# Edge attention on one Trainium2 core: one operand of VectorE in PSUM, edge loads spread over other rounds, and one multiplication of the counting loop given to GpSimd

## What is computed

```python
h = jnp.einsum('ni,hio->hno', x, W)                      # 4 heads of 64
e = attn_src[:, src_idx] + attn_dst[:, dst_idx]
e = jnp.where(e >= 0, e, NEG_SLOPE * e) * edge_weight[None, :]
e_exp = jnp.exp(e - jnp.max(e))
denom = jax.ops.segment_sum(e_exp.T, dst_idx, num_segments=num_nodes).T
alpha = e_exp / (denom[:, dst_idx] + 1e-10)
msg = h[:, src_idx] * alpha[..., None]
out = jax.vmap(lambda m: jax.ops.segment_sum(m, dst_idx, num_segments=num_nodes))(msg)
x = x + out                                              # summed by destination, added to x
```

## Time and profile before

| what | value |
|---|---|
| time, median of 3 runs | 5204.59 us (5191.33 to 5204.67) |
| the profiled execution's own time | 5195.46 us |
| its span, first to last instruction | 5193.8 us |
| TensorE busy | 4168.2 us (80%) |
| VectorE busy | 2408.1 us (46%) |
| GpSimd busy | 862.5 us (17%) |
| mean granted TensorE clock | 0.883 |

### The profile page before, as it was taken

The page is one execution under the profiler, slowest core; times in us unless marked ns, Lnnn a source line. Parts: engine busy times, 40 slices in busy tenths (PEclk is TensorE's granted clock), DMA queues, the critical chain, the costliest instruction groups (busy, mean ns, idle before and its releaser), DMA issues. The chain is left out here.

```text
span 5193.8 us, 79246 instructions
## 1 busy us (share of the span) xinstructions
PE 4168.2 (80%) x22693; PEld 3605.1 (69%) x22694; DVE 2408.1 (46%) x4239; ACT 1855.3 (36%) x3178; POOL 862.5 (17%) x796
## 2 busy tenths in 40 slices
PE   2588877955749976967997998997499969899675
PEld 2476767954638843866886886886499858788554
DVE  5355558965340032126995995897411140110424
ACT  2333323642410032424664664665143310110322
POOL 2577770002600010210000000000122200000101
PEclk8688888986969988988998998998599979999788
DMA  3344432542343211321221221221312144133000
GB/s 102 84 114 116 121 90 98 214 172 64 107 140 148 86 33 38 125 72 41 57 54 33 58 57 32 54 56 24 91 60 80 51 132 159 75 150 148 13 18 27
DMA packets 459231, 440.36 MB, mean 85 GB/s; under 512 B 347128, under 2 KB 411341, under 8 KB 446050
## 3 DMA queue, kind: packets, MB, share of 16 engines
q1 hardware_dynamic: 423868, 341.36, 21.6%
q0 software_dynamic: 35232, 97.61, 6.5%
HBM read 342.44 MB, written 96.42 MB: 84 GB/s over the span
## 5 line engine op out<-in xcount | busy, mean ns | idle before, releaser
L2575 PE MATMUL p_acc<-p_H,p_eT 125*125 125x256 f32 x3750 | 823.6, 379 | 0.0
L2575 PEld LDWEIGHTS p_acc<-p_H,p_eT 125*125 125x125 f32 x3750 | 696.2, 187 | 105.0
L1120 POOL DMA_INDIRECT p_message<-edge_table,p_index x425 | 495.1, 1165 | 170.5 <-issue 119.5
L1371 PE MATMUL p_acc<-p_message,p_spread 125*125 125x260 f32 x1666 | 427.9, 424 | 33.9 <-issue 29.1
L2059 DVE BATCH_NORM_STATS2 features_stats<-F x60 | 29.2, 487 | 868.0 <-ACT F L2050 867.3
L1371 PEld LDWEIGHTS p_acc<-p_message,p_spread 125*125 125x125 f32 x1666 | 349.9, 212 | 104.1 <-issue 36.2
L1830 ACT ACTIVATE p_hid<-p_up,p_b1s 128x125 f32<-128x125 f32 x764 | 272.2, 365 | 398.4 <-PE p_up L1806 355.0
L1806 PEld LDWEIGHTS p_up<-p_xT,p_w1s 128*128 128x128 f32 x3056 | 377.6, 199 | 50.1 <-issue 33.8
L1806 PE MATMUL p_up<-p_xT,p_w1s 128*128 128x125 f32 x3056 | 385.0, 284 | 32.0 <-issue 14.0
L1814 PE MATMUL p_down<-p_w2s,p_hid 128*125 128x256 f32 x1528 | 361.3, 386 | 11.7 <-ACT p_hid L1830 10.5
L526 PE MATMUL p_turned<-identity,p_slot 125*128 125x125 f32 x400 | 89.1, 376 | 303.3 <-DVE p_slot L494 299.7
(11 more groups left out here) (492 smaller groups left out, 6794.8 us busy)
## 6 DMA issues: line engine op xcount, KB each, us to landing
sums_first<-edge_sums SPq DMA_DIRECT2D x39, 1562.5 KB
p_count<-edge_counts SPq DMA_DIRECT2D x375, 152.6 KB
p_second<-edge_sums SPq DMA_DIRECT2D x36, 1562.5 KB, 8.0
edge_sums<-p_sums SPq DMA_DIRECT2D x25, 1562.5 KB
edge_counts<-p_total SPq DMA_DIRECT2D x25, 683.6 KB
p_w1s<-in_L_ffn_W SPq DMA_DIRECT2D x16, 1024.0 KB
p_got<-made SPq DMA_DIRECT2D x25, 560.0 KB
p_dst_all<-dst_row SPq DMA_DIRECT2D x25, 531.2 KB
```

Source lines behind the costliest of these rows:

```text
L1120: pool.indirect_dma_start(message[:, m, k, :], None, table, bass.IndirectOffsetOnAxis(ap=index[:, m, k:k + 1], axis=0)).then_inc(landed[m] ...
L1371: last = pe.matmul(at, spread[:, k], message[0:P, m, k], start=(k == 0), stop=(k == R_CH - 1))
L2575: last = pe.matmul(acc[:, s, 0:C], eT[:, r % 4, a % 4], H[:, a, 0:C], start=(a == 0), stop=(a == T - 1))
```

## The change

The change has these parts. (a) In `attend_edges` VectorE reads one operand of L1255 and L1283 from PSUM: the destinations are copied there once (`dst_of`), and ScalarE writes the exponentials a second time, to `raise_of`. (b) SP issues the block loads of a round three rounds later, behind that round's `dst_all`; there are 660 instead of 630. (c) `begin_rest`, `pick_rest`, the first six steps and the last six of `block_keys` stand behind rounds 18, 19, 21 and 22. (d) The two closing instructions over 125 x 6400 are gone; in the counting loop VectorE does the same for one tile of 256 features behind every fifth batch, through `attended`. (e) In the counting loop `heavy` is computed by GpSimd, and `low` is 125 wide instead of 128. (f) The last loop loads and stores 5 columns for each of 25 slices of `old_sums` instead of whole rows.

```diff
-LOADED = 21
-HELD = LOADS * LOADED
+SETS = 3
+HELD = LOADS * ((CH // (CH // T)) - SETS)
...
+def block_lows(dve, then, own):
+
+
+    then(dve.tensor_copy(own.spare, own.edges[:, 0:BLOCKS, 1]))
     then(dve.tensor_scalar(own.base, own.spare, 4195.0, None, ALU.mult))
     then(dve.tensor_copy(own.spare_i, own.base))
     then(dve.tensor_scalar(own.spare_i, own.spare_i, 19, None, ALU.arith_shift_right))
     then(dve.tensor_copy(own.base, own.spare_i))
     then(dve.scalar_tensor_tensor(out=own.low, in0=own.base, scalar=-float(P), in1=own.spare, op0=ALU.mult, op1=ALU.add))
-    then(dve.tensor_copy(own.spare, dst))
+
+
+def block_keys(dve, then, own, based):
+
+
+    then(dve.tensor_copy(own.spare, own.edges[:, 0:BLOCKS, 0]))
...
-        low = ph.sb("low", [EB, SLOTS, KB, ROWS])
+        low = ph.sb("low", [EB, SLOTS, KB, P])
...
+        old_sums = ph.sb("old_sums", [P, T, BLK])
...
-        old_sums = sums[0:P, 1]
...
-            eng.tensor_tensor(heavy[:, at], low[:, at], own.edges[:, bass.ds(n * KB, KB), 2:3].bitcast(F32).to_broadcast([EB, KB, ROWS]),
+            eng.tensor_tensor(heavy[:, at, :, 0:P], low[:, at], own.edges[:, bass.ds(n * KB, KB), 2:3].bitcast(F32).to_broadcast([EB, KB, P]),
                               ALU.mult).then_inc(heavy_ready, 1)
+
+        @block.gpsimd
+        def _(pool):
+            over_batches(pool, lambda n, k, i: weighs(pool, n, k))
 
 
         @block.vector
         def _(dve):
             dve.sem_inc(batch_summed, SLOTS)
+            dve.memset(heavy[:].rearrange("p s b l -> p (s b) l")[:, :, P:ROWS], 0.0).then_inc(cleared, 1)
             dve.sem_inc(counts_kept, TURNS)
             dve.sem_inc(batch_kept, TURNS)
 
...
-                dve.tensor_tensor(low[:, at], lanes(ROWS), each(own.low, n, ROWS), ALU.is_equal).then_inc(low_ready, 1)
+                dve.tensor_tensor(low[:, at], lanes(P), each(own.low, n, P), ALU.is_equal).then_inc(low_ready, 1)
                 dve.tensor_tensor(cell[:, at], lanes(P), each(own.key, n, P), ALU.is_equal).then_inc(cell_ready, 1)
-                weighs(dve, n, k)
-
-            over_batches(dve, one)
...
+
+            def one_and_tile(n, k, i):
+                one(n, k, i)
+                if k % IN_GROUP == IN_GROUP - 1:
+                    t = i * (PER // IN_GROUP) + k // IN_GROUP
+                    o = attended[0][:, tile(t), 0:C].rearrange("p a (h o) -> p (a h) o", h=HEADS)
+                    dve.tensor_tensor(o, o, attended[1][:, tile(t), :].rearrange("p a h -> p (a h)").unsqueeze(2).to_broadcast([P, HEADS, HO]), ALU.mult).then_inc(shared, 1)
+                    dve.wait_ge(shared, t + 1)
+                    x = X[:, tile(t), :].rearrange("p a c -> p (a c)")
+                    dve.tensor_tensor(x, x, attended[0][:, tile(t), 0:C].rearrange("p a c -> p (a c)"), ALU.add)
+
+            over_batches(dve, one_and_tile)
...
+                then(dve.tensor_tensor(old_sums[:], old_sums[:],
                                        acc[0:P, 0, 1, 0, 0:P].rearrange("p (d h) -> p h d", h=T), ALU.add))
...
+                old = weights.rearrange("r (h d) -> r h d", h=T)[bass.ds(group * ROWS, P), :, bass.ds(place * BLK, BLK)]
+                sp.dma_start(old_sums[:], old).then_inc(old_loaded, 16)
...
+                sp.dma_start(old, old_sums[:]).then_inc(rest_stored, 16)
...
-        total = ph.sb("total", [P, T, W])
-        den = ph.sb("den", [P, T, HEADS])
+        total, den = attended
...
+        dst_of = ph.psum("dst_of", [P, 512])
+        raise_of = ph.psum("raise_of", [P, 512])
...
-            with eng.Fori(0, ROUNDS // SETS - 1) as i:
+        def over_pipeline(eng, one, single=1):
+            with eng.Fori(0, ROUNDS // SETS - single) as i:
...
-            for r in range((ROUNDS // SETS - 1) * SETS, ROUNDS):
+            for r in range((ROUNDS // SETS - single) * SETS, ROUNDS):
...
             sp.wait_ge(loops_made, 4)
-            for r in range(SETS):
-                blocks_of(r)
-            with sp.Fori(1, LOADED // SETS) as i:
+            with sp.Fori(1, ROUNDS // SETS) as i:
                 for m in range(SETS):
                     one(i * SETS + m, i, m)
-                    blocks_of(i * SETS + m)
-            for r in range(LOADED, ROUNDS):
+                    blocks_of((i - 1) * SETS + m)
+            for r in range(ROUNDS // SETS * SETS, ROUNDS):
                 one(r, r // SETS, r % SETS)
+                blocks_of(r - SETS)
...
-                act.activation(message[0:P, m, :, C:W], logit[:], ACT.Exp, bias=minus[:, m:m + 1]).then_inc(raised, 1)
+                act.activation(message[0:P, m, :, C:W], logit[:], ACT.Exp, bias=minus[:, m:m + 1])
+                act.activation(raise_of[:, 0:R_CH * HEADS], logit[:].rearrange("p k h -> p (k h)"), ACT.Exp, bias=minus[:, m:m + 1]).then_inc(raised, 1)
...
+            dve.tensor_copy(dst_of[:, 0:CH + PAD], g.dstf[:]).then_inc(dst_kept, 1)
+            dve.wait_ge(dst_kept, 1)
...
                     dve.tensor_tensor(spread[:, lo:lo + n], g.iota[:, nodes(t)].unsqueeze(1).to_broadcast([P, n, P]),
-                                      g.dstf[:, bass.ds(r * R_CH + lo, n)].unsqueeze(2).to_broadcast([P, n, P]),
+                                      dst_of[:, bass.ds(r * R_CH + lo, n)].unsqueeze(2).to_broadcast([P, n, P]),
                                       ALU.is_equal).then_inc(spread_ready, 1)
...
                     o = rows_of[:, :, 0:C].rearrange("p k (h o) -> p k h o", h=HEADS)
-                    dve.tensor_tensor(o, o, rows_of[:, :, C:W].unsqueeze(3).to_broadcast([P, n, HEADS, HO]), ALU.mult).then_inc(scaled, 1)
+                    dve.tensor_tensor(o, o, raise_of[:, lo * HEADS:(lo + n) * HEADS].rearrange("p (k h) -> p k h", h=HEADS).unsqueeze(3).to_broadcast([P, n, HEADS, HO]), ALU.mult).then_inc(scaled, 1)
...
+            rest_then = Steps(dve, rest_setup)
...
                 one(r, i, m, coming)
-                then = Steps(dve, rest_setup, 0 if coming == 2 else 16)
+                if coming == 6:
+                    begin_rest(dve, rest_then, g, own_blocks.low[0:1], own_blocks.spare_i[0:1], own_blocks.spare[0:1, 0:1])
+                if coming == 5:
+                    pick_rest(dve, rest_then, g, own_blocks.low[0:1])
+                if coming == 3 and isinstance(r, int):
+                    dve.wait_ge(own_edges_loaded, 16 * HELD)
+                    block_lows(dve, rest_then, own_blocks)
                 if coming == 2:
-                    over = own_blocks.low[0:1]
-                    begin_rest(dve, then, g, over, own_blocks.spare_i[0:1], own_blocks.spare[0:1, 0:1])
-                    pick_rest(dve, then, g, over)
-                if coming == 1:
-                    dve.wait_ge(own_edges_loaded, 16 * HELD)
-                    block_keys(dve, then, own_blocks, based)
-
-            over_pipeline(dve, one_and_blocks)
+                    block_keys(dve, rest_then, own_blocks, based)
+
+            over_pipeline(dve, one_and_blocks, single=2)
...
-            o = total[:, :, 0:C].rearrange("p t (h o) -> p t h o", h=HEADS)
-            then(dve.tensor_tensor(o, o, den[:].unsqueeze(3).to_broadcast([P, T, HEADS, HO]), ALU.mult))
-            then(dve.tensor_tensor(X[:], X[:], total[:, :, 0:C], ALU.add))
```

More of the change, by code:

```diff
@@ L787, in __init__ @@
         self.spare_i = at[4].bitcast(I32)
-def block_keys(dve, then, own, based):
-    src, dst = (own.edges[:, 0:BLOCKS, k] for k in (1, 0))
-    then(dve.tensor_copy(own.spare, src))
+def block_lows(dve, then, own):
+    then(dve.tensor_copy(own.spare, own.edges[:, 0:BLOCKS, 1]))
     then(dve.tensor_scalar(own.base, own.spare, 4195.0, None, ALU.mult))
@@ L805, in block_keys, with count_edges @@
     then(dve.tensor_copy(own.lane, own.lane_i))
-def count_edges(nc, g, edges, own, counts, weights):
+def count_edges(nc, g, edges, own, attended, X, counts, weights):
     SLOTS = 5
@@ L839, in count_edges @@
         sums_stored = [ph.sem(f"sums_stored{m}") for m in range(2)]
+        shared = ph.sem("shared")
+        cleared = ph.sem("cleared")
         rest_read = ph.sem("rest_read")
@@ L934, in one @@
                     for q in range(many):
-                        last = pe.matmul(at_bank[0:P, 0, bank, q * P:(q + 1) * P], cell[:, at, first + q], low[:, at, first + q, 0:P], start=True, stop=True)
+                        last = pe.matmul(at_bank[0:P, 0, bank, q * P:(q + 1) * P], cell[:, at, first + q], low[:, at, first + q], start=True, stop=True)
                 last.then_inc(batch_counted, 1)
@@ L1029, with attend_edges @@
 FROM = 3
-SETS = 3
 PIECES = ((0, 5), (5, 4), (9, 4), (13, 4))
-def attend_edges(nc, g, table, a_dst, dst_flat, dst_row, edges, own_blocks, X):
+def attend_edges(nc, g, table, a_dst, dst_flat, dst_row, edges, own_blocks, attended):
     W = C + HEADS
@@ L2928, in build @@
                 own_blocks = Blocks(XT)
-                attend_edges(nc, g, edge_table, a_dst, d["dst_flat"], dst_row, d["edges"], own_blocks, X)
```

(5 more changed lines are left out.)

8 lines of the change are left out of this document (2 added, 6 removed).

## The result

| what | before | after |
|---|---|---|
| time, median | 5201.89 us (4 runs, 5191.33 to 5204.67) | 5160.49 us (4 runs, 5158.9 to 5163.23) |
| ratio of after to before | | 0.9933, 95% interval 0.9921 to 0.9944 |
| span of the profiled execution | 5193.8 us | 5157.2 us |

A forecast was written before the change was run, and what follows sets the result against it. GpSimd's gathers were taken to bound the attention narrowly over TensorE; TensorE and VectorE were both full in counting. Terms −36.5 − 32 − 13.7 + 1 + 92 − 5 = +5.8 us gave 5205 us, range 5150 to 5250.

The forecast's parts named there:

- The likeliest case: Whole kernel: exclusion at 2.8 to 3.0 us a counting batch cancels the attention's gain, 5189 to 5220 us; chance 0.36.
- the counting loop: Counting stage: VectorE and GpSimd exclude each other, so 125 batches cost +92 us (bounds +50 and +137).
- the last loop: End of the stage: loading a 25th of old_sums in 3125 small pieces gives −5 us (bounds −13 and +10).
- the price of a batch: Counting loop: a batch takes 2.94 us instead of 2.20, the engines' work added up (2.86 to 3.13).
- The cheap case: Counting loop: starts overlap, a batch is 2.6 to 2.75 us, or 10 us more comes elsewhere; 5159 to 5185; chance 0.20.
- The argument that I gave for the lower end: Counting loop: each instruction's fixed part (decoding, semaphores) need not be exclusive, so 2.94 us within 2.86 to 3.13.
- SP's order: Attention's first rounds: destinations issued ahead of the edges remove ScalarE's 36.53 us wait, −36.5 us (bounds −30 and −41).
- the bound of −30: Attention's first rounds: the smallest gain forecast from issuing destinations earlier, if the gathers stay slow.
- One operand in PSUM: Attention: VectorE no longer holds GpSimd's gathers, which fall from 1165 to 947 ns; −32 us (bounds 0 and −37).
- the row of 4.90 us: Attention trace before: VectorE's two-SBUF-operand message scaling, read as one instruction holding a 2.25 us gather for about its length.
- Block work: Attention's late rounds: in four pieces, part of TensorE's 11.33 and 4.80 us waits goes, part returns; +1 us (bounds −10, +8).
- Closing instructions: After the attention: nothing ran beside the two removed instructions, so −13.7 us, 2 × 6.83.

The follow-up runs named there:

- the block work late: Changed kernel with begin_rest and pick_rest behind round 22 again and all of block_keys behind round 23: 5157.36 us, ratio 0.9923 to the kernel before.
- the doubled multiplication: Changed kernel with GpSimd making the same multiplication twice a batch, first into a buffer nobody reads: 5279.51 us, ratio 1.0165 to the kernel before.

## Why the prediction went wrong

The forecast was no change that can be told, 5205 us; the measured time is 0.67% under before, in the range but in another case. The likeliest case and the measured one differ by the terms of the loops, not by the mechanisms: of the 42.4 us between the forecast sum, +5.8, and the measured −36.6, the counting loop has 37.1 and the last loop 5.6.

- **The step that failed: the price of a batch, "I take 2.94".** It measured 2.67 on average: 2.48 for four batches and some 3.4 for the fifth, with its tile instructions. The exclusion was there as described (the operand in PSUM takes it away, the second multiplication doubles it). What was mis-sized is GpSimd's part. I took the whole length of its records from a later layer, 1.29 to 1.50 us; 2.94 is 1.46 for VectorE, 1.34 for GpSimd and 0.14 for the tiles. An undisturbed multiplication takes 1.24 us, and it keeps VectorE out for 1.03 of them; the rest of its record, and all that is above 1.24, lies beside VectorE's own work. 2.94 became 1.45 + 1.03 + 0.95/5 = 2.67. The whole loop before has 278.7/125 = 2.23 us a batch, not the 2.20 of its steady rows, so 125 batches cost +54.9 us instead of +92. The cheap case (2.6 to 2.75, chance 0.20) named this result; its range of 5159 to 5185 held the time, at its lower edge. The argument that I gave for the lower end, that a part of each instruction need not be exclusive, should have moved the number more than it did.
- **SP's order**: −36.1 against −36.5; both late things, ScalarE's tiles and the landing of messages, came where the working had them (178.0 and 177.5, measured 178.37). By itself it gives 32, since the gathers then stay slow and round 1 starts at 184.63: the bound of −30 in the prediction.
- **One operand in PSUM**: mechanism right, gathers at 950 ns. The stretch to round 18's visits gave −24.9 and not −32, because I put the whole gain there. VectorE's waits for messages were 24.7 us in rounds 1 to 17 and 9.6 behind, and those behind counted too: with the gathers freed and the block work late, the stretch from round 18's visits to the counting fell from 185.9 to 165.1 us, 7.0 more than the closing instructions account for. Added to the new order alone the operand is worth 35.1 us, near the forecast. My reading of the earlier trace rows was too long by four: the row of 4.90 us is four instructions of 1.22, and the gather of 2.25 us is 1.30 over the median, so it was held for about one of them. The rule of the Trainium skill, "SBUF — State Buffer", section "Who interferes with whom", on one SBUF input is borne out (1157 ns with two, 950 with one operand in SBUF). By the inference of the Trainium skill, same section, that `tensor_tensor` leaves the generation of DMA descriptors alone these gathers would not have been held, and they were; they also read their indices (`p_index`) from SBUF, and no run tells whether that or the descriptors were kept waiting. The Trainium skill has the lock there for the whole instruction; the doubled multiplication shows 1.03 of the 1.24 us of its record.
- **Block work**: +1 forecast, and undone it is 1 to 3 us faster by the medians, within what this comparison tells. **Closing instructions**: TensorE's wait ahead of the counting fell from 20.83 to 7.10 us, −13.7 as forecast. The attention as a whole came out at −81.7 against −81.2; the errors of its two later stretches, +7 and −8 us, cancel, and the operand's gain behind round 18, which I had put ahead of it, is nearly all of both.
- **The parts together**: measured one at a time they fall short of the 81.7 by 14 us (32.0 for SP's order in the kernel before, 22.1 for the operand in the changed kernel, 13.7 for the closing instructions, nothing for spreading). Added one after the other they come to it: 32.0 + 35.1 + 13.7 + 1.0 = 81.8. What stays open is why spreading with the gathers held also gained some 5 us ahead of round 18.
- **The last loop**: −10.6 against −5; the small pieces were no brake, and whole rows give all of it back (41.0 against 30.0 us).

## What to carry to other kernels

A full engine's work given to an idle one was no gain here, where both read two operands from SBUF and shut each other out: it cost about 40 us although GpSimd was idle and TensorE was the bound. Moving the work back gave 5118 us; the better remedy was to put one small broadcast operand of VectorE in PSUM (5107 us). Price such an exclusion by what is added to the other engine's period, in a stretch where the two meet, and not by the length of the records, which hold the waiting too. Two parts of a change that shorten the same waits do not add: spreading the block work was worth 14 us with the gathers held and 1 with them free, so the parts measured one at a time fell 14 us short of the whole.

## What was not expected of the hardware

The two engines that shut each other out take turns, instruction by instruction, and neither starves: in the kernel with the doubled multiplication each one-hot of VectorE is followed by a multiplication of GpSimd, at 3.51/2 = 1.76 us a pair. The record of such an instruction holds its wait as well: VectorE's 0.80 reads as 1.84, 1.04 more, and GpSimd's 1.24 as 1.62 to 1.80. The loads of the last loop had landed 6.7 us after the first issue with 3125 pieces of 20 bytes (1098.80 to 1105.51), and 14.5 us after it with 125 rows of 12.5 KB (1100.61 to 1115.11).
